# First graph layer: rows found by matmul without their score, the score made by VectorE

## The reference

```python
h = jnp.maximum(_layernorm(x, axis=-1), 0.0)
s_src = h @ attn_w[:d]
s_dst = h @ attn_w[d:]
e = s_src[src] + s_dst[dst]
e = jnp.where(e >= 0, e, LEAKY_SLOPE * e)
m = segment_max(e, dst); ex = jnp.exp(e - m[dst])
alpha = ex / segment_sum(ex, dst)[dst]
out = segment_sum(h[src] * alpha[:, None], dst)
x = x + out
```

## Time and profile before

| | |
|---|---|
| median of 3 runs | 7915.2 us (7913.37 to 7917.22) |
| the profiled execution | 7915.85 us |
| its span, first to last instruction | 7914.0 us |
| PE busy | 5415.2 us, 68% |
| DVE busy | 5484.0 us, 69% |
| POOL busy | 5700.7 us, 72% |
| ACT busy | 2058.4 us, 26% |
| mean granted TensorE clock | 0.827 of full speed |
| first layer's loop | 601 to 3519 us of the span |

### The profile page before, as it was taken

One profiled execution on the slowest core, in us unless ns is written; L12 is line 12 of the kernel. 1 busy time (PEld: TensorE's weight loads), 2 busy tenths in 40 slices (PEclk: granted clock), 3 DMA queues, 4 the chain that ended last, 5 costly groups with the idle time before them and its releaser, 6 DMA issues.

```text
span 7914.0 us, 77431 instructions
## 1 busy us (share of the span) xinstructions
PE 5415.2 (68%) x27115; PEld 2803.9 (35%) x27148; DVE 5484.0 (69%) x8259; ACT 2058.4 (26%) x3765; POOL 5700.7 (72%) x6014
## 2 busy tenths in 40 slices
PE   0009999999999999976756555655555555555553
PEld 0005555555555555543322222222222222222223
DVE  8437766776677667765557777777777777777772
ACT  0000100110011001115633344333334333333441
POOL 5777777777777777745357777777777777777776
PEclk9999999999999999988877666666666666666665
DMA  4412222222222222228965555555555555555552
GB/s 106 115 45 52 50 58 48 48 52 56 48 48 56 51 48 48 58 56 338 396 213 165 165 165 169 166 163 165 164 165 165 167 168 164 165 163 164 165 168 61
DMA packets 392057, 995.10 MB, mean 126 GB/s; under 512 B 171574, under 2 KB 220003, under 8 KB 371060
## 3 DMA queue, kind: packets, MB, share of 16 engines
q0 software_dynamic: 244128, 525.43, 28.3%
q1 hardware_dynamic: 147539, 464.72, 15.9%
HBM read 593.27 MB, written 395.35 MB: 125 GB/s over the span
## 4 chain that ended last, share of the span: by engine, by line
PE 30%; DVE 28%; POOL 22%; DMA 10%; issue 9%; ACT 1%; DVEq 0%; POOLq 0%; SPq 0%; ACTq 0%
PE ps L1008 28%; POOL arena L708 20%; DVE arena L1560 9%; DMA arena<-layer_rows,edge_row_index 6%; DMA layer_rows<-arena 3%; DVE arena L1522 2%; DVE aggregate_nodes L1520 2%; DVE arena L1555 2%; DVE arena L1351 2%; DVE h_nodes L1359 2%; DVE arena L1335 2%; DVE ps L1327 1%; DVE h_nodes L1554 1%; POOL dst_score_at_starts L744 1%; DVE arena L1362 1%
## 5 line engine op out<-in xcount | busy, mean ns | idle before, releaser
L708 POOL DMA_INDIRECT arena<-layer_rows,edge_row_index x5508 | 5218.1, 947 | 1768.0 <-issue 1717.4
L1008 PE MATMUL ps<-arena 128*128 128x396 bf16 (+1 forms) x10752 | 2736.6, 336 | 0.0
L1008 PE MATMUL ps<-h_nodes,arena 128*128 128x396 bf16 (+1 forms) x5376 | 1806.4, 336 | 0.0
L1095 PE MATMUL ps<-arena,weights_and_zeros 128*128 128x384 bf16 (+1 forms) x2144 | 818.3, 382 | 1195.5 <-ACT aggregate_nodes L929 1195.5
L1008 PEld LDWEIGHTS ps<-arena 128*128 128x128 bf16 x10752 | 1044.1, 98 | 784.7 <-issue 18.8
L1359 DVE TENSOR_TENSOR h_nodes<-ps,h_nodes 128x429 f32<-128x429 f32 x672 | 604.9, 900 | 808.7 <-PE ps L1008 808.7
L1560 DVE COPY_PREDICATED arena<-ps,arena 128x3072 f32<-128x3072 uint32 (+2 forms) x405 | 904.1, 2232 | 29.3 <-DVE arena L1522 1.8
L1095 PE MATMUL ps<-h_nodes,weights_and_zeros 128*128 128x384 bf16 (+1 forms) x2144 | 815.5, 380 | 0.0
L1095 PE MATMUL ps<-weights_and_zeros 128*128 128x384 bf16 (+1 forms) x2144 | 808.5, 377 | 0.0
L1095 PEld LDWEIGHTS ps<-arena,weights_and_zeros 128*128 128x128 bf16 x2144 | 237.1, 111 | 1429.9 <-ACT aggregate_nodes L929 1230.9
L1008 PEld LDWEIGHTS ps<-h_nodes,arena 128*128 128x128 bf16 x5376 | 523.8, 97 | 405.5 <-issue 9.1
(11 more groups left out here) (283 smaller groups left out, 6621.1 us busy)
## 6 DMA issues: line engine op xcount, KB each, us to landing
layer_rows<-arena SPq DMA_DIRECT2D x98, 1601.5 KB, 8.2
layer_scans<-weights_and_zeros SPq DMA_DIRECT2D x134, 768.0 KB, 4.1
arena<-layer_rows,edge_row_index POOLq DMA_INDIRECT x5508
layer_scans<-arena SPq DMA_DIRECT2D x52, 1054.0 KB, 4.2
y_in_h_at_starts<-weights_and_zeros SPq DMA_DIRECT2D x52, 1023.0 KB
weights_and_zeros<-y_in_h_at_starts SPq DMA_DIRECT2D x134, 396.0 KB, 4.1
layer_rows<-weights_and_zeros SPq DMA_DIRECT2D x49, 64.0 KB
edge_row_index<-row_of_edge SPq DMA_DIRECT2D x134, 12.0 KB
```

Source lines behind the costliest of these rows:

```text
L708: pool.indirect_dma_start(tile, None, table, bass.IndirectOffsetOnAxis(ap=index, axis=0)) \
L1008: ins = nc.tensor.matmul(found[col % 2][:, 0:wide], onehot[n % 2][:, a, c * P:(c + 1) * P], tparts[i][:, a, 0:wide], start=a == 0 and i == ...
L1095: ins = nc.tensor.matmul(found1[e][:, 0:wide * D], onehot1[:, a, e * P:(e + 1) * P], rows, start=a == 0 and i == 0, stop=a == LOWS - 1 and ...
```

## The change

The rows that TensorE finds are 32 numbers long and leave the score out: `FP` is 32 in place of 33, the table parts, the product and the sum of a pick go by the features alone, and a pick writes `g0` from `H0` on. The matmuls are 416 and 384 wide. The source score of the 14 found columns is then made in `scores0`, in groups 4 to 51, behind the wait for the gathered columns and ahead of the sum of the two scores: a product of the 14 x 32 features with the attention weights, written into columns 48 to 61 of the PSUM tile `b0t`, and a sum over the 32 into the score's place. `b0t` is overwritten later in the same iteration by `weigh0`. The 48 gathered columns still bring their score along.

```diff
-FP = D + 1
+FP = D
-TW = HIGHS * FP + 1
+TW = HIGHS * FP
@@ scores0
                 v.wait_ge(s_g0[u], landed0(g))
+                if g >= NB:
+                    by_weight = by_edge(b0t)[:, KP:K, :]
+                    w = wattn[:, 0:D].unsqueeze(1).to_broadcast([P, PC, D])
+                    done(v.tensor_tensor(by_weight, g0[u][:, KP:K, H0:H0 + D], w, ALU.mult))
+                    done(v.tensor_reduce(g0[u][:, KP:K, S0], by_weight, AX.X, ALU.add))
                 done(v.tensor_tensor(e0, g0[u][:, :, S0], sdst_e[:, at], ALU.add))
@@ pick
-                done(v.tensor_reduce(g0[g % NB][:, KP + i, 0:FP], picked[col % 2],
+                done(v.tensor_reduce(g0[g % NB][:, KP + i, H0:H0 + FP], picked[col % 2],
                                      AX.X, ALU.add))
@@ the table parts, once
-            tab_wide = tab[:, wide, 0:FP].rearrange("p (b a) c -> p a b c", a=LOWS)
-            tab_tall = tab[:, tall, 0:FP]
+            tab_wide = tab[:, wide, H0:H0 + FP].rearrange("p (b a) c -> p a b c", a=LOWS)
+            tab_tall = tab[:, tall, H0:H0 + FP]
```

## The result

The changed kernel takes 7965.1 us (median of 6 runs, 7957.6 to 7969.3) against 7916.2 (7913.4 to 7919.5) for the kernel before on the same chip: ratio 1.006, 95% interval 1.0049 to 1.007. That is 49 us or 0.6% slower; the forecast was 7945, the range 7920 to 7970. The profiled execution took 7960.1 us, its span is 7958.3, 44.3 longer than before.

A forecast was written before the change was run, and what follows sets the result against it. TensorE's columns and VectorE's chain were taken to bound the first-layer loop in turn. From 7915.9 us, work -6.2 (-63.4 - 5.2 + 62.4) and clock +36 gave 7946, against the median 7945; range 7920 to 7970.

The forecast's parts named there:

- What bounds the loop: First-layer loop, 2918 us: TensorE's columns and VectorE's chain in turn; two groups take 22 columns plus 29.04 us of VectorE.
- -63.4 for TensorE: First-layer columns on the path: narrower multiplies take 3.99 us per column, 0.12 less, over 24 x 22 columns.
- Sum of the work: First-layer loop without the clock: -63.4 TensorE, -5.2 picks, +62.4 new product and sum; together -6.2 us.
- The new pair: Product and sum in VectorE's scores, groups 4 to 51: 1.30 us with waits, 48 times, +62.4 us.
- rival 2: VectorE's new sum and product pay extra for strided PSUM, 0.58 us x 48 = +28: 7978 us. Chance of full price 0.08.
- The pauses: TensorE's waits for one-hot rows grow from 2.13 to 3.8 us and 1.29 to 2.8, total 85 to some 155.
- The clock: Behind first-layer pauses TensorE's low clock follows 46, at 1.3 us each, against 14 x 1.68 today: +36 us.
- The dearer price: First-layer low-clock stretches behind pauses at half the throttled time: 48 cost 82 us instead of 59.8, making the total +52.
- Rival 1: In the loop the clock falls no more often than today, so -6 remains: 7909 us, same. Chance 0.14.
- Rival 3: TensorE's pauses swallow VectorE's new product and sum, so -63 to -69 stays: 7850 us. Chance 0.03.
- Rival 4: TensorE's first-layer multiplies do not get cheaper with the width, +63: 8008 us. Chance 0.02.
- Costed at nothing: GpSimd's gathers (52 us of cover), ScalarE's exponentials, table parts, final loop, tail and second layer: no change in time.

The follow-up runs named there:

- the two filled kernels: Kernel before with repeated multiplies ahead of long pauses, 7890.3 us; changed kernel with them ahead of both kinds of pause, 7879.0 us; same chip, kernel before 7912.2.
- the filled one: Changed kernel with repeated, unneeded multiplies ahead of TensorE's last column before each pause: 7882.8 us against 7912.4 for the kernel before, ratio 0.9961.
- the pair alone: Kernel before plus only the new product and sum, rows still 33 wide: 8027.4 us against 7912.4; with pauses filled 7952.6, +62.3 over the filled kernel before.
- the narrow rows alone: Changed kernel without the new product and sum, found columns' score left out: 7863.3 us against 7912.4 for the kernel before, ratio 0.9937.

## Why the prediction was right, and where not

- **What bounds the loop: right.** The path is TensorE's columns and VectorE's chain in turn; each half alone, with the clock taken out, came within 1.3 us of what was expected once a column of the changed kernel had been measured at 3.98 us (62.3 for 61, 73.7 for 73). The prediction's own -63.4 for TensorE was 5 too small, since its column of 3.99 and 0.12 were rounded from single starts; 0.13 x 528 is 68. Sum of the work: forecast -6.2, measured -11.3 between the two filled kernels (-15 by their loops without the low clock left in one).
- **The new pair: right,** 1.25 us of work and 1.30 on the path. The dearer sum (rival 2) is refuted: 626 ns for 448 strided elements out of PSUM. By the Trainium skill ("SBUF — State Buffer", section "Door 1: The DMA port swizzle"), as the prediction read it, each step to a new PSUM line would have been paid for. This case's trace does not agree, for VectorE; the page's own sentence on PSUM speaks of matmuls only, and no run here tests those.
- **The pauses: right.** 2.8 to 2.9 and 3.8 to 3.9 us against 2.8 and 3.8; the total 159.7 against 155. In the kernel before, the low clock followed 14 of 23 pauses of 2.1 us; the prediction's 24th, the first, was 1.75 us long.
- **The clock: the mechanism right, the term mis-sized.** Forecast 46 x 1.3 - 23.5 = +36; measured 80.6 - 23.6 = +57, which is outside the bounds the prediction gave this term (18 to 54). Three things went into it. Fewer pauses than assumed were followed by a low stretch, 41 against 46. The single ones were priced nearly right: 28 cost 42.8 us, 1.53 each for the forecast's 1.3. "Behind a pause of 3.8 us about 1 us of it falls into the pause" holds for 14 of the 21 long pauses in question (0.65 to 1.26 us), but behind the other 7 the whole stretch lay behind the restart. The step that failed is that every stretch was taken to be as long as the one of rows 6: 13 were twice as long and cost 2.7 to 3.0 us, 37.8 in all, which nothing in the trace before had shown. Had all 41 been single at 1.53, the term had been 63 - 24 = +39.
- **The total.** Work and clock together are -11 (or -15) + 57 = 42 to 46 us, against 43.3 in the loop. That 7965 lies inside the range is in part luck: the work came out 5 to 9 us below its term and took back a part of the 21 us by which the clock was above.
- **The dearer price.** The Trainium skill, "TensorE: Matmul & The Clock Gate" ("HAM oscillation — how this bites in real kernels"), charges half of the throttled time at every restart. By that the prediction made the stretches 82 us and the total +52, so 7967; measured 80.6 us and 7965. Half of the throttled time is right, here too: 3.41 us at the low clock behind a restart cost 1.69. That the sum fits is luck: it stands for 48 single stretches, and there were 28 single and 13 double ones, with 20 us of them inside pauses.
- **Rivals.** Rival 1 (clock unchanged) fell with the changed kernel's own trace, and the filled one showed the link. Rival 2 fell with the sum's 626 ns. Rival 3 (the pair swallowed by the pauses) fell with the pair alone, +62 where the clock is out of it. Rival 4 (width without effect) fell with the narrow rows alone, -49.
- **Costed at nothing: mostly right.** In the three last groups I counted the pair fully. Only the first paid: from the start of its scores to the next they take 12.72, 12.71 and 12.71 us, where they took 11.38, 12.65 and 12.64; in the later two VectorE waited for ScalarE anyway. It is 1.5 us in place of 3.9. The 52 us of cover of GpSimd held for the change and became the floor once the loop was faster.

## What to carry to other kernels

When two engines take turns on the path, an instruction added to the one lengthens the other's pause, and on TensorE that can cost more than the instruction: here 1.3 us of VectorE work cost 1.3 us of path and about 1 us more of clock (pair alone: 72.9 - 23.6 = 49 us over 48 groups). Look for the place in the same program where the engine already waits, and put the work there; if a pause of two microseconds or more can't be avoided, TensorE can be given useless multiplies in a part of it. And before counting on a gain, look which engine ends next: here 52 us of cover on GpSimd capped it.

## What the runs showed of the hardware

- A pause of TensorE between 1.3 and 1.6 us never lowered its clock here (165 cases), 2.1 us did in 14 of 23, 2.5 to 2.6 us in 35 of 46 without the pair, and 2.6 to 4.3 us in 175 of 180 with it. Pauses of 4.1 to 4.3 us cost hardly more each (1.7 us, and 2.3 in 10 of 45) than those of 2.6 to 2.7 (1.6 to 1.7).
- Useless multiplies made a kernel faster: 537 of them took the changed kernel from 49 us over the kernel before to 30 under it.
- The low clock often begins while TensorE still stands, and that part of it costs nothing. A low stretch that began 0.79 us or more before the restart was twice as long as the others (28 of 28); of the others none began more than 0.77 us before it. What puts its beginning there was not settled.
- A sum that reads 448 numbers of PSUM at a stride of 63 took VectorE 626 ns, no more than an unstrided one by size; out of SBUF at a stride of 32, 416 took 854 ns where the unstrided sum of a pick takes 586.
